# A graph network's message stream in two parts: the first added up inside the second's loop, and three accumulating scatters in eight instead of four

## What is computed

```python
h = relu(layernorm(x))
agg = segment_sum(h[src], dst) / max(counts, 1)
x = x + log_softmax(agg @ W_l.T + h @ W_r.T + b)
h = relu(layernorm(x))
weight = maximum(edge_attr_64 @ W1 + b1, 0.0) @ W2 + b2
hn = h @ Wl + bl
x = x + segment_sum(hn[dst] * weight, src)
```

## Time and profile before

| | |
|---|---|
| median of 3 runs | 4332.68 us (4325.3 to 4332.99) |
| the profiled execution | 4327.8 us, of which the span is 4325.7 us |
| mean granted TensorE clock | 0.83 |
| PE, DVE, ACT, POOL busy | 85%, 60%, 43%, 52% of the span |
| HBM traffic | 468 MB, 108 GB/s over the span |

### The profile page before, as it was taken

One profiled execution on the slowest core, in us unless ns is written; L12 is line 12 of the kernel. 1 busy time (PEld: TensorE's weight loads), 2 busy tenths in 40 slices (PEclk: granted clock), 3 DMA queues, 4 the chain that ended last, 5 costly groups with the idle time before them and its releaser, 6 DMA issues.

```text
span 4325.7 us, 91322 instructions
## 1 busy us (share of the span) xinstructions
PE 3658.2 (85%) x24740; PEld 2560.7 (59%) x24741; DVE 2598.5 (60%) x7184; ACT 1858.2 (43%) x3754; POOL 2263.1 (52%) x1753
## 2 busy tenths in 40 slices
PE   1899999998788888888888888888888888778887
PEld 1666666666555555555555555555555555467776
DVE  8888888887744444444444444444444444367776
ACT  3666666664422222222222222222222222278887
POOL 2100000001488888888888888888888888800000
PEclk9999999998877677776777777777777777699999
DMA  3499800000244454554555555444555445478787
GB/s 91 151 328 321 306 5 6 5 4 1 51 83 83 82 83 83 83 82 83 83 83 83 82 83 83 83 83 83 83 83 83 83 83 83 70 204 225 225 225 210
DMA packets 491789, 468.65 MB, mean 108 GB/s; under 512 B 64152, under 2 KB 476198, under 8 KB 491733
## 3 DMA queue, kind: packets, MB, share of 16 engines
q1 hardware_dynamic: 342150, 348.90, 30.6%
q0 software_dynamic: 149584, 119.07, 19.1%
HBM read 235.79 MB, written 231.94 MB: 108 GB/s over the span
## 4 chain that ended last, share of the span: by engine, by line
PE 26%; issue 25%; DVE 18%; POOL 13%; DMA 13%; DVEq 3%; ACT 1%; POOLq 0%; ACTq 0%; another core or an unknown queue 0%; SPq 0%
POOL messages L502 13%; DMA messages<-big,idxr 12%; PE PS L1001 11%; PE PS L992 4%; PE PS L1141 4%; DVE X L926 3%; PE PS L1177 3%; DVE aux L680 2%; DVE big L887 2%; PE PS L1129 1%; DVE big L864 1%; DVE big L861 1%; DVE H L915 1%; DVEq L921 1%; PE PS L1118 1%
## 5 line engine op out<-in xcount | busy, mean ns | idle before, releaser
L502 POOL DMA_INDIRECT messages<-big,idxr x1664 | 2139.1, 1286 | 541.8 <-issue 430.2
L881 DVE CAST idxr<-big 128x4 int32<-128x4 f32 x416 | 109.9, 264 | 1281.4 <-DMA messages<-big,idxr 1267.1
L1141 PE MATMUL PS<-par,big 128*128 x4992 | 686.1, 256 | 115.7 <-issue 105.6
L1141 PEld LDWEIGHTS PS<-par,big 128*128 128x128 bf16 x4992 | 497.6, 101 | 359.0 <-issue 229.0
L1129 PE MATMUL PS<-W2s,big 128*128 128x128 f32 x3328 | 685.8, 370 | 0.0
L1001 PE MATMUL PS<-par,aux 128*128 128x386 bf16 x3626 | 682.2, 327 | 0.0
L1129 PEld LDWEIGHTS PS<-W2s,big 128*128 128x128 f32 x3328 | 582.3, 263 | 132.7 <-issue 132.7
L1321 ACT ACTIVATE big<-PS 128x512 f32<-128x512 f32 x416 | 248.5, 597 | 856.2 <-PE PS L1141 803.8
L1239 ACT ACTIVATE aux<-PS 128x784 bf16<-128x784 f32 x592 | 480.0, 822 | 294.7 <-PE PS L992 286.0
L1177 PE MATMUL PS<-big,H 128*128 128x128 f32 x3456 | 444.4, 282 | 98.9 <-DVE H L915 96.1
L455 POOL DMA_INDIRECT KLg<-edge_keys,tj_i x37 | 73.9, 1997 | 795.3 <-PE PS L972 767.5
(11 more groups left out here) (213 smaller groups left out, 4009.8 us busy)
## 6 DMA issues: line engine op xcount, KB each, us to landing
messages<-zeros SPq DMA_DIRECT2D x576, 193.5 KB
big<-messages SPq DMA_DIRECT2D x216, 516.0 KB, 3.8
aux<-slot_rows SPq DMA_DIRECT2D x416, 128.0 KB
big<-in_edge_attr_dram SPq DMA_DIRECT2D x402, 128.0 KB
messages<-big,idxr POOLq DMA_INDIRECT x1664
X<-in_x_dram SPq DMA_DIRECT2D x6, 448.0 KB, 12.2
out_dram<-X SPq DMA_DIRECT2D x6, 448.0 KB
edge_places<-big SPq DMA_DIRECT2D x1, 2496.0 KB, 13.3
```

The lines of the kernel that those rows point to most:

```text
L502: pool.indirect_dma_start(strm_d, bass.IndirectOffsetOnAxis(ap=idxr[:, n % U, j:j + 1], axis=0), outr[:, n % U, j, :], None, compute_op=AL ...
L1141: last = nc.tensor.matmul(pHG[:, j * C:(j + 1) * C], oht[:, k % 2, j * P:(j + 1) * P], h1p[:, ds(at + a * C, C)], start=(a == 0), stop=(a ...
```

## The change

The stream is cut into two parts. Groups 0 to 208 (GA = 209) scatter into segments 0 to 123 (OA = 124), groups 209 to 415 into the 116 segments behind them (OB). Each part has its own bucket starts, from its own half of the histogram, so that the blocks' buckets occur twice and there are 240 segments instead of 216.

The 124 segments of the first part are added up inside the steps of the second: two steps in each three, from step 214 on, carry a segment. SP loads it, after waiting once for the scatters of the first 209 groups; ScalarE and VectorE build its one-hot matrices; TensorE multiplies at the end of its step into a single PSUM bank `pFL`; and VectorE adds the sums one step later, ahead of its messages. To free that bank the ranks use one bank instead of two, and TensorE computes those of group s + 1 after the gathers of group s. The tail does the last 116 segments as before.

Of each eight scatters the second, fifth and eighth accumulate. The zeros cover more rows (NZ = 682), and the block list is loaded ahead of the loop.

```diff
+    GA = 209
+    TA = GA * J
+    OA = 124
+    OB = -(-(NS - TA + 2 * NB) // FO)
+    OB += -OB % 4
+    NOCT = OA + OB
+    CAP = NOCT * FO + P - 2
...
+        pQ = PS[:, 6, 0:5 * NBK].rearrange("p (j b) -> p j b", j=5)
+        pFL = PS[:, 7, :]
...
+        L_A, L_B = 17, 15
+        S_A = U + L_A * 3 * U
+        S_B = S_A + 3 * U
+        FIRST_OCTS = {S_A + 6: 0, S_A + 7: 1, S_A + 9: 2, S_A + 10: 3}
...
+            with eng.Fori(0, L_B) as i:
+                for k in range(U * rings):
+                    m = k - k // 3 if k % 3 < 2 else None
+                    step(i * (U * rings) + (S_B + k), S_B + k, None if m is None else (i * 8 + (4 + m), 4 + m))
...
+            def first_part_landed():
+                for k in range(U):
+                    sp.wait_ge(S_sc[k], 64 * len(range(k, GA, U)))
...
-                                            outr[:, n % U, j, :], None, compute_op=ALU.add if j % 2 == 1 else ALU.bypass).then_inc(S_sc[n % U], 16)
+                                            outr[:, n % U, j, :], None, compute_op=ALU.add if (n * J + j) % 8 in (1, 4, 7) else ALU.bypass).then_inc(S_sc[n % U], 16)
...
+            def pair_blocks():
+                nc.vector.tensor_copy(starts[:, 0, NB:], starts[:, 1, NB:])
+                link(nc.vector.tensor_scalar(extra[:, 3:4], iotaP[:, 0:1], float(PA), None, ALU.is_ge))
+                link(nc.vector.tensor_tensor(split, starts[:, 1, 1:NB], starts[:, 0, 1:NB], ALU.subtract))
+                link(nc.vector.scalar_tensor_tensor(out=split, in0=split, scalar=extra[:, 3:4], in1=starts[:, 0, 1:NB], op0=ALU.mult, op1=ALU.add))
...
+            def layer1(s, n, o):
+                more = not isinstance(s, int) or s + 1 < G
+                if not isinstance(s, int) or s + 2 < G:
+                    block_hot(s + 2, n + 2)
+                if more:
+                    one_hot_T(s + 1, n + 1)
+                if o:
+                    stream_hot(*o)
+                if adding[0]:
+                    block_adds(adding[0][0], pFL)
+                adding[0] = o
+                messages(s, n)
+                if more:
+                    row_places(s + 1, n + 1)
...
+            def layer1(s, n, o):
                 k = n % U
                 known = isinstance(s, int)
                 node_rows(s, k)
+                if not known or s + 1 < G:
+                    ranks(s + 1, n + 1)
                 weights(s, k)
                 if not known or s + 1 < G:
                     hidden(s + 1, (k + 1) % U)
                 if not known or s + 2 < G:
                     attr_T(s + 2, (k + 2) % U)
-                    ranks(s + 2, n + 2)
+                if o:
+                    wait(pe, S["fadd_done"], o[0] * (FO // 2))
+                    sums(*o, pFL)
```

More of the change, by code:

```diff
@@ L270, in gnn_program, with steps @@
         assert U == 4
[L272 removed]
+        L_A, L_B = 17, 15
+        S_A = U + L_A * 3 * U
+        S_B = S_A + 3 * U
+        FIRST_OCTS = {S_A + 6: 0, S_A + 7: 1, S_A + 9: 2, S_A + 10: 3}
+        assert S_A + 1 == GA and S_B + L_B * 3 * U + 4 * U == G and OA == 4 + 8 * L_B
+        def steps(eng, step, turn=None, rings=3):
             for s in range(U):
[L275 to L276 removed]
+                step(s, s, None)
+            with eng.Fori(0, L_A) as i:
                 for k in range(U * rings):
[L278 to L280 removed]
+                    step(i * (U * rings) + (U + k), U + k, None)
+            if turn:
+                turn()
+            for s in range(S_A, S_B):
+                step(s, s, (FIRST_OCTS[s],) * 2 if s in FIRST_OCTS else None)
+            with eng.Fori(0, L_B) as i:
+                for k in range(U * rings):
+                    m = k - k // 3 if k % 3 < 2 else None
+                    step(i * (U * rings) + (S_B + k), S_B + k, None if m is None else (i * 8 + (4 + m), 4 + m))
+            for s in range(S_B + L_B * U * rings, G):
+                step(s, s, None)
         def attr_landed(g, k):
@@ L925, in block_adds, with second_part @@
                     wait(dve, S["fadd_done"], i * (FO // 2) + r)
-                    nc.vector.tensor_tensor(Xf[:, ds(at, C)], Xf[:, ds(at, C)], pF[:, n % 4, r * C:(r + 1) * C], ALU.add)\
+                    nc.vector.tensor_tensor(Xf[:, ds(at, C)], Xf[:, ds(at, C)], sums[:, r * C:(r + 1) * C], ALU.add)\
                         .then_inc(S["fadd_done"], 1)
+            adding = [None]
+            def layer1(s, n, o):
[12 more added lines that the diff above has]
+                    row_places(s + 1, n + 1)
+            def second_part():
+                dve.wait_ge(S["rank_chain"], 5 * GA)
+                link(nc.vector.tensor_copy(taken[:, 0:NB], starts[:, 1, 0:NB]))
+                dve.wait_ge(S["bq_in"], 16)
+            steps(dve, layer1, second_part)
             def segment(i, n):
@@ L1154, in _, with sums @@
             ranks(0, 0)
-            ranks(1, 1)
-            def layer1(s, n):
+            def sums(i, n, to):
+                k = n % 4
+                pe.wait_ge(S["finhot_ready"], i + 1)
+                pe.wait_ge(S["acthot_ready"], i + 1)
+                for r in range(FO // 2):
+                    for q in range(2):
+                        last = nc.tensor.matmul(to[:, r * C:(r + 1) * C], finhot[:, n % 2, r * 2 + q, :], fin[:, k, r, q * ROW:q * ROW + C],
+                                                start=(q == 0), stop=(q == 1))
+                last.then_inc(S["finmm_done"], 1)
+            def layer1(s, n, o):
                 k = n % U
```

136 lines of the change are left out of this document (60 added, 76 removed).

## The result

| | before | after |
|---|---|---|
| median | 4328.99 us (4324.4 to 4332.99) | 4101.88 us (4085.5 to 4110.19) |
| the profiled execution | 4327.8, span 4325.7 | 4110.19, span 4108.4 |
| mean granted TensorE clock | 0.83 | 0.874 |

The ratio is 0.947 (95% interval 0.944 to 0.951): the change takes 227 us off. That is faster, as forecast, but 109 us above the predicted 3993 and 17 above the upper end of the range. The gain should have been 340 us (4332.7 - 3993); a third of it is missing.

The account below looks back on a forecast made before the run. GpSimd issuing scatters was taken to set the loop's step, 6.36 us. 4325.7 - 120.6 - 235.8 + 10 + 5 + 3.8 + 1 = 3989.1 us of span, stated as 3993 us; range 3968 to 4085.

Parts of the forecast that it names:

- The scatters, -120.6: Loop: one accumulating scatter in eight becomes plain, saving 0.58 us 208 times; step 6.07 us in both halves.
- Rival 2: Loop scatters: a plain one right behind a plain one costs as much as an accumulating one; +241 us, about 4235; chance 0.05.
- The tail, -235.8: Tail after the loop: 100 fewer segments than 216, at 2.36 us each.
- GpSimd held by a busier VectorE, +10: Loop's second half: scatters lengthened by VectorE's added work, 0.05 us a step for 207 steps.
- Rival 3: Loop: GpSimd starves beside a busier VectorE; +147 us, about 4140; chance 0.06.
- Clock and TensorE, +5: Loop's second half: TensorE's clock changing level could cost 0 to 68 us; 5 taken.
- rival 4: Loop's second half: TensorE stays at 1.2 GHz, 9.24 us a step; slower than before, about 4650; chance 0.04.
- Ranks, +0, and the waits of the one bank, +0: Loop: earlier ranks in one bank, and products waiting about 1 us for additions one step in three, cost nothing.
- The start, +4.8: Counting stage and loop entry: one more scan and eight operations, 3.8 us; new code and copied starts, +1.
- None of these costs time while the lead is there: Loop's second half: added waits inside a step cost nothing, given 12 us of lead over GpSimd.
- Rival 1: Loop's second half: waits between VectorE, TensorE and one bank make 6.4 to 6.7 us a step; about 4085; chance 0.15.
- What would show it: Signs: right, loop about 2540 us, clock above 0.85; wrong, message-ended gaps, second-half step over 6.2, cast not waiting for scatters.

Follow-up runs that it names:

- sets C, E and F: Later sets of runs in which the kernel after ran again, unchanged: 3983.98, 3985.94 and 3981.9 us.
- the first run: The kernel after as measured for the result: 4101.88 us, ratio 0.947 to the kernel before.
- set C: Kernel after, unchanged: 3983.98 us; kernel before with only three accumulating scatters in eight instead of four: 4203.68 us.
- The mix alone: Kernel before with only the scatters changed, three accumulating in eight instead of four: 4200.84 us, later again 4203.68 us.
- The ranks alone: Kernel before with only the rank products changed, one PSUM bank and ahead of the edge weights: 4318.61 us, ratio 0.9987.
- the first set of runs: The result's own runs: kernel before 4328.99 us, kernel after 4101.88 us.
- sets B to F: All sets after the first and set A: variants of the kernel after, itself unchanged, and the mix alone again; 3619.44 to 4203.68 us.
- set B: Kernel after with four accumulating in eight for groups 208 to 399, 4033.66; additions behind messages, 4125.68; additions on 8 columns, 3983.73; quarter loads, 3981.0 us.
- set A: Kernel before with mix alone 4200.84 or ranks alone 4318.61; kernel after with register load moved 4108.84 or two of sixteen products a segment 4049.29 us.
- the kernel made for it: Kernel after with four accumulating scatters in each eight, in pairs, two accumulating then two plain: 4134.76 us.
- The two that had both mixes: Kernel after with four accumulating scatters in eight from group 208 to 399, three elsewhere, run twice: 4033.66 and 4033.46 us.

## Why the prediction came out as it did

It was wrong for the result above: the kernel took 109 us more than forecast. For the same program in sets C, E and F it was 7 to 11 us too high. The sum of the span was 3989.1; those sets have 3985.5, 3985.7 and 3975.9. Term by term, by the first run and set C:

- **The scatters, -120.6.** Right. The mix alone gave -122.9 and -123.9 (4203.68 against 4327.60). Rival 2, that a plain scatter behind a plain one costs 1.87, fell: with plain scatters only, all 1664 in a row, the first half is at 5.13 / 4 = 1.28.
- **The tail, -235.8.** Right. It went from 535.0 to 300.2 us, -234.8, in both runs.
- **GpSimd held by a busier VectorE, +10.** Right in size, not in cause. In set C the second half takes (3685.3 - 2415.2) / 207.75 = 6.11 us a step against 6.06 in the first, 11 us in all. The scatters themselves grew, from 1.210 to 1.226 us in the mean, and four times that is the 0.06. But with additions on 8 columns the second half still has 6.12 against 6.04, so the width of the additions is not it. That agrees with SBUF — State Buffer of the Trainium skill, "Who interferes with whom", which has tensor_tensor keep off the port that descriptors are written through (the page calls this inferred), for this part of the new work; what makes the 0.05 us is open, since a quarter of the loads leaves it too (6.14 against 6.04) and the comparisons of the segments were not tried. Rival 3, at 147 us, falls even so.
- **Clock and TensorE, +5.** Nothing of it shows in the pace, since GpSimd leads. The granted clock in the second half is 0.91 in set C, as forecast, against 0.80 from 1200 to 2400 us, and rival 4 fell.
- **Ranks, +0, and the waits of the one bank, +0.** Right. The ranks alone are within 0.3% of before.
- **The start, +4.8.** The first scatter came 8.1 us later than before in the first run (1154.6 against 1146.5) and 8.2 in set C, and from 1148.5 to 1158.6 in the other kernels with the same counting stage; the 3.4 us between are within that. One scan is 2.02 us by the row (994.82 + 0.18 - 992.98) and not 2.06, which changes nothing.

**The step that failed** is the one below the second half: "None of these costs time while the lead is there". The sum let every engine start as soon as its input was computed, within some 0.05 us of it, because the waits of the kernel before gave little reason to think otherwise (9 late copies of 377, by at most 0.67 us). In the first set of runs results of TensorE reached the others up to 4 us after their end. In the first half that was free: GpSimd had its groups ready and the step stayed at 6.06. In the second half it was not. The kernel without accumulating scatters tells how much room that half has: its engines manage 5.3 to 5.4 us a step with every result in time, so at 6.07 there are some 0.7 us to lose. The late starts added about 1.4 us (6.81 against 5.4), of which 0.7 came out at the end. That is an estimate from two kernels whose granted clocks differ in this stretch (0.88 with late starts, 0.95 without accumulating scatters), not measured by itself; the 0.70 a step by which the messages held GpSimd is measured. Over 176 steps (6.81 - 6.12) that is 121 us, and the whole difference of the two times is 118. That the lead over GpSimd was 12 us for the places was read rightly; but the messages are formed last, and their lead is eaten by each step that takes longer than 6.07, so that a lead protects only from single delays. The prediction should have compared the chain's own step with GpSimd's, and it had no row of that chain with a segment in it.

**Rival 1** had the right sign and nearly the right time, 4085, and all the marks that "What would show it" set out as wrong were there: a step over 6.2 in the second half with 6.07 in the first, gaps that end with the messages, the cast no longer waiting. But its mechanism, waits among VectorE, TensorE and the one bank, was not it by itself. In sets B to F the same waits are there and cost nothing at this pace. Had the study ended with set B, I would have called the mix the cause and a slower mix the remedy, and both are wrong where no start is late: there the slower mix costs 50 us.

Additions behind the messages are the one edit that makes the waits of rival 1 real, without any late start: 6.92 us a step. From 2500 to 3700 us TensorE then waits for the additions before its sums, and GpSimd for the messages (us in total, times, longest):

```profile
PE PS L1208 <- DVE X L949: 101.2, 58, 1.9
...
POOL messages L532 <- DVE big L922: 158.0, 93, 3.3
```

So the place of the additions ahead of the messages matters, 142 us against the kernel after in set C, and the change had it right.

**What stays open** is what makes the starts late. It is not a property of the kernel after: the unchanged program had none in three later sets. It is not one of the chip or set alone either: in set A, on one chip, the three kernels with three accumulating scatters in eight had 85 to 124 late relus each in these stretches, and the one with four in eight had 4, none over 0.55 us. Traces of it are there even so: ScalarE's copy of the node rows was over 0.5 us late in 26 of 377 steps, up to 1.4 us, and in the first trace of the kernel before in 9, up to 0.67, against none in set C. Whether the pace or plain scatters in a row call them up could not be told, since the kernel made for it met a set without them. The two that had both mixes never met such a set, so that nothing here shows how the slower mix, or plain scatters only, fare there.

Two things in the traces narrow it down. First, only TensorE's signals are seen to be late: in the first half of the loop of the first run (1200 to 2400 us) 85 relus and 91 copies start over 0.5 us late, but none of the 150 rank products for which TensorE waited on VectorE is over 0.15 us late, and no scatter has a gap over 0.32. The record of the late signal, where there is one (83 of the 85 relus), is late too: in that run and the mix alone it stands 0.02 us before the relu in the median. So it is the signal that comes late, not the relu that starts late after it. Second, the two sets with late starts are the two whose traces lack records. The engines raise the loop's semaphores 7904 times in every kernel. The traces of sets B to F have 7844 of these records or more. Those of the first set have 4714 (after) and 5285 (before), and those of set A 4473 to 5806, the fewest with three accumulating scatters in eight. So the first thing to suspect is the recording itself, or something that holds up both TensorE's signals and the records. No run here tells these apart, since every execution comes with a recorded span and clock. Whether the 118 us would be there without a recording is not shown. Loss of records is not enough by itself: the kernel before lost a third of them and took its usual time.

## What to carry to other kernels

When the time of a change misses the sum, run the same program again on another chip before explaining it. Here three edits seemed to cure the loss, and only the unchanged kernel told that the chip or the set was the difference. A stretch whose code is the same in all variants serves as the witness of its set at no cost. So does the number of semaphore records in the trace: where a third is missing, as in the first trace here, its releasers are not to be relied on, and the time wants a second run before it is explained.

Slack in a loop has two parts: the lead, which absorbs one delay, and the difference between the leader's step and the followers' own, which absorbs a delay in every step. Work that is moved under cover uses up the second, and it is then that disturbances which were free before come out at the end.

Ask of a costly form whether it is needed at all before mixing it more thinly. The accumulating scatters added to zeros; none of them was needed, and leaving all of them out gave another 360 us.

## What the runs showed of the hardware

- ScalarE's relu was let go up to 4.4 us after TensorE's product ended, and VectorE's messages at the same time for a different product, with "remote" as the releaser on a kernel of one core. In the first run, from 1200 to 2400 us, no rank product of TensorE was over 0.15 us late on VectorE's results. Late relus came in two of seven sets of runs. In those sets they were, with three accumulating scatters in eight, 31 to 86 of some 200 steps in the first half and of 27 to 54 of 176 in the second; with four, at most 3, by 0.55 us. Both sets' traces hold 57% to 73% of the loop's semaphore records, all others over 99%.
- A scatter of 128 rows with 129 floats takes GpSimd 0.96 to 0.99 us plain and 1.56 to 1.61 accumulating (medians by mix: 1.56 where the two alternate, 1.59 with three in eight, 1.61 in pairs), with 0.30 between, plain ones in an unbroken row included. From four in eight to none the loop's first half went 6.36, 6.06, 5.74, 5.41, 5.13 us a step.
- Loading 129 KB instead of 516 KB a segment left the time within 1 to 5 us (3981.0, against 3981.9 to 3985.9 in other sets): with the DMA share at 0.69 in the second half and 0.51 with the smaller loads, the pace was the same.
